# A language-model tower in four blocks: blocks that end without GpSimd's queue drain, and setup's folded weight products reordered

## The reference

```
table = where(is_num, sin(num_value/1000 * freqs), weight);  h = table[x]
q, k, v = split(layernorm(h) @ Wq, @ Wkv)                    # 8 heads of 64
dots = (q k^T) * scale;  dots[diagonal] = -1e-9;  dots = mix(dots, mix_pre)
h = h + (mix(softmax(dots), mix_post) v) @ Wout + bout
y = layernorm(h)
h = h + gelu(y Ws1 + bs1) Ws2 + bs2 + bank_sp(y) + bank_fq(y)  # a bank: top-1 of 8 experts, capacity 1280
```

## Time and profile before

| what | value |
|---|---|
| median of three runs | 1586.62 us |
| the profiled execution | 1587.35 us |
| its span (first to last instruction) | 1585.6 us |
| TensorE busy | 1496.5 us, 94% |
| ScalarE, VectorE, GpSimd busy | 1156.2, 1085.5, 1023.7 us |

### The profile page before, as it was taken

How to read it: one execution, slowest core, us unless ns; L and a number is a source line. 1 busy time by engine, 2 the same in 40 slices (tenths; PEclk the granted TensorE clock), 3 DMA queues, 4 the chain that set the end, 5 groups by cost and what they waited for, 6 DMA issues and landing times. The chain is left out here.

```text
span 1585.6 us, 33983 instructions
## 1 busy us (share of the span) xinstructions
PE 1496.5 (94%) x11213; PEld 1381.3 (87%) x11213; DVE 1085.5 (68%) x2864; ACT 1156.2 (73%) x3447; POOL 1023.7 (65%) x1068
## 2 busy tenths in 40 slices
PE   5549999999999999999999999987999999699999
PEld 2248999999999999999999999977999999699999
DVE  6757787787887887877878787752333333288887
ACT  5539888888888888888888888854555555355554
POOL 5856557878878878878788787663756655422221
PEclk9869999999999999999999999998999999899999
DMA  6323221221211111100000000002334334244444
GB/s 233 131 92 115 96 70 52 69 68 48 59 57 46 56 55 50 46 27 15 14 14 15 15 15 7 4 5 52 83 99 101 84 74 116 64 140 129 131 128 114
DMA packets 157790, 110.59 MB, mean 70 GB/s; under 512 B 28115, under 2 KB 145341, under 8 KB 157616
## 3 DMA queue, kind: packets, MB, share of 16 engines
q1 hardware_dynamic: 140208, 88.25, 18.6%
q0 software_dynamic: 17408, 20.16, 4.6%
HBM read 54.23 MB, written 70.17 MB: 78 GB/s over the span
## 5 line engine op out<-in xcount | busy, mean ns | idle before, releaser
L918 ACT ACTIVATE expd<-masked,nmax 128x128 f32<-128x128 f32 x1024 | 396.0, 393 | 0.0
L729 POOL TENSOR_TENSOR prob<-expd,rtotal 128x1024 f32<-128x1024 f32 x128 | 243.0, 1898 | 143.8 <-DVE rtotal L996 142.9
L1013 DVE COPY_PREDICATED masked<-off_diag,ps_s 128x1024 f32<-128x1024 int32 x128 | 174.9, 1366 | 149.4 <-PE ps_s L816 149.4
L858 PE MATMUL ps_o<-u,probT 128*128 128x128 f32 x2048 | 249.2, 275 | 0.7 <-issue 0.7
L858 PEld LDWEIGHTS ps_o<-u,probT 128*128 128x128 f32 x2048 | 239.1, 192 | 0.9 <-issue 0.9
L918 ACT ACTIVATION_READ_ACCUMULATOR expd<-masked,nmax 128x1 f32 x1024 | 197.0, 192 | 0.0
L927 ACT ACTIVATE u<-ps_ut 128x1024 f32<-128x1024 f32 x128 | 131.4, 1027 | 67.8 <-PE ps_ut L869 67.8
L1028 DVE TENSOR_TENSOR w_lo<-ps_w,w_hi 128x512 fp32r<-128x512 f32 x256 | 164.4, 681 | 5.8 <-ACT w_hi L948 5.8
L941 ACT ACTIVATE probT<-ps_ut 128x1024 f32<-128x1024 f32 x128 | 131.5, 1028 | 45.0 <-PE ps_ut L824 38.3
L948 ACT ACTIVATE w_hi<-ps_w 128x512 fp32r<-128x512 f32 x256 | 146.5, 596 | 19.4 <-PE ps_w L846 12.7
L1019 DVE TENSOR_REDUCE nmax<-masked 128x8 f32<-128x1024 f32 x128 | 155.5, 1214 | 2.5
(11 more groups left out here) (228 smaller groups left out, 4074.9 us busy)
## 6 DMA issues: line engine op xcount, KB each, us to landing
answers_sp<-zeros SPq DMA_DIRECT2D x16, 512.0 KB
answers_fq<-zeros SPq DMA_DIRECT2D x16, 512.0 KB
sh_back<-answers_sp SPq DMA_DIRECT2D x56, 128.0 KB, 2.4
sh_back<-answers_fq SPq DMA_DIRECT2D x56, 128.0 KB, 2.4
out<-res SPq DMA_DIRECT2D x56, 128.0 KB, 1.9
h_sb<-in_L_tok_weight SPq DMA_DIRECT2D x12, 512.0 KB, 5.4
table<-h_sb SPq DMA_DIRECT2D x12, 512.0 KB
sent_sp<-zeros SPq DMA_DIRECT2D x8, 660.0 KB, 3.0
```

The lines of the kernel that those rows point to most:

```text
L729: nc.gpsimd.tensor_tensor(prob[k % 2][:, :].rearrange("p (g j) -> p g j", g=H), expd[k % 2][:, :].rearrange("p (g j) -> p g j", g=H), rtot ...
L858: mm = nc.tensor.matmul(ps_o[:, 0:D], probT[k % 2][:, g * N:(g + 1) * N], u[k % 2][:, g * D:(g + 1) * D], start=(g == 0), stop=(g == H - 1))
L918: ins = nc.scalar.activation(expd[(k - 1) % 2][:, g * N:(g + 1) * N], masked[(k - 1) % 2][:, g * N:(g + 1) * N], ACT.Exp, bias=nmax[(k - 1 ...
L1013: nc.vector.copy_predicated(masked[k % 2][:, :].rearrange("p (g j) -> p g j", g=H), off_diag[:, :].unsqueeze(1).to_broadcast([P, H, N]), p ...
```

## The change

All four blocks are opened with `no_gpsimd_drain=True`. The block's end then has no drain instruction on GpSimd. The other four engines still drain, and then count up the semaphore with an instruction of its own; GpSimd waits for four counts and releases all, as before.

In setup, M is now summed half by half: steps c = 5 to 12 each hold one product of 512 columns instead of steps 5 to 8 holding two, and step 11 no longer holds the first product of N. N's eight products all stand behind the last step, and go to two other accumulators, `ps_t` and `ps_c`, one half in each. They wait for the copy of `ids` out of `ps_c` (made in VectorE's step 6), and no longer for `M_lo`. `M_hi` and `M_lo` move from inside the loops of ScalarE and VectorE to behind them, and `N_hi` and `N_lo` are made in halves of 512 columns.

```
-        block = s.enter_context(nc.Block())
+        block = s.enter_context(nc.Block(no_gpsimd_drain=True))      # in all four blocks

 # ScalarE
-                for w in range(2):
-                    if c == (10, CHUNKS + 1)[w]:
-                        act.wait_ge(S["M"], w + 1)
-                        nc.scalar.activation(mats["MN"[w] + "_hi"][:, :], ps_m[:, :], ACT.Copy).then_inc(S["hi"], 1)
+            act.wait_ge(S["M"], 2)
+            nc.scalar.activation(mats["M_hi"][:, :], ps_m[:, :], ACT.Copy).then_inc(S["hi"], 1)
+            for half, src in enumerate((ps_t, ps_c)):
+                act.wait_ge(S["M"], 3 + half)
+                nc.scalar.activation(mats["N_hi"][:, half * 512:(half + 1) * 512], src[:, :], ACT.Copy).then_inc(S["hi"], 1)

 # TensorE
+            def product(w, c, half):
+                pe.wait_ge(S["wT_out"], 2 + w)
+                pe.wait_ge(S["mixed"], w * HC + c + 1)
+                if w:
+                    pe.wait_ge(S["coef"], 3)
+                dst = (ps_t, ps_c)[half][:, :] if w else ps_m[:, half * 512:(half + 1) * 512]
...
-                if 5 <= c < 5 + HC:
-                    product(c - 5)
-                if c == 11:
-                    product(HC)
-            for c in range(HC + 1, 2 * HC):
-                product(c)
+                if 5 <= c:
+                    product(0, (c - 5) // 2, (c - 5) % 2)
+            for c in range(HC):
+                for half in range(2):
+                    product(1, c, half)

 # VectorE
-                if c == 10:
-                    low(0)
             put_sines(CHUNKS - 2)
             put_sines(CHUNKS - 1)
-            low(1)
+            dve.wait_ge(S["hi"], 1)
+            link.inc(nc.vector.tensor_tensor(mats["M_lo"][:, :], ps_m[:, :], mats["M_hi"][:, :].bitcast(F32), ALU.subtract))
+            for half, src in enumerate((ps_t, ps_c)):
+                at = slice(half * 512, (half + 1) * 512)
+                dve.wait_ge(S["hi"], 2 + half)
+                link.inc(nc.vector.tensor_tensor(mats["N_lo"][:, at], src[:, :], mats["N_hi"][:, at].bitcast(F32), ALU.subtract))
             link.wait()
```

More of the change, by code:

```diff
@@ L281, in setup @@
         names = ("made", "num", "num_f", "numT", "numT_out", "angle", "whole", "reduced", "clamped", "sine", "done", "put",
-                 "weights", "wT", "wT_out", "coef", "coefd", "coef_out", "mixed", "M", "hi", "lo")
+                 "weights", "wT", "wT_out", "coef", "coefd", "coef_out", "mixed", "M", "hi")
         S = {n: sem("s_" + n) for n in names}
@@ L487, in coefficients @@
                 nc.tensor.transpose(ps_c[:, 256:384], idx_f[:, :], ident[:, :]).then_inc(S["coefd"], 1)
[L489 to L502, removed]
+            def product(w, c, half):
[4 more added lines that the diff above has]
+                dst = (ps_t, ps_c)[half][:, :] if w else ps_m[:, half * 512:(half + 1) * 512]
+                ins = nc.tensor.matmul(dst, (wkT, wvT)[w][:, c, :], mixed[:, w * HC + c, half * 512:(half + 1) * 512],
+                                       start=(c == 0), stop=(c == HC - 1))
+                if c == HC - 1:
                     ins.then_inc(S["M"], 1)
@@ L575, in put_sines @@
                                           angle[c % 3][:, 0:n * D].rearrange("p (r d) -> p r d", r=n)).then_inc(S["done"], 1)
[L577 to L580, removed]
             for c in range(CHUNKS):
@@ L587, in _ @@
                     dve.wait_ge(S["coef_out"], 2)
-                    link.inc(nc.vector.tensor_copy(ids[:, :], ps_c[:, 256:384]))
+                    nc.vector.tensor_copy(ids[:, :], ps_c[:, 256:384]).then_inc(S["coef"], 1)
                     dve.wait_ge(S["made"], made["rank_i"])
                     link.inc(nc.vector.tensor_copy(C.rank[:, :], C.rank_i[:, :]))
-                if c == 10:
-                    low(0)
             put_sines(CHUNKS - 2)
             put_sines(CHUNKS - 1)
-            low(1)
+            dve.wait_ge(S["hi"], 1)
[4 more added lines that the diff above has]
+                link.inc(nc.vector.tensor_tensor(mats["N_lo"][:, at], src[:, :], mats["N_hi"][:, at].bitcast(F32), ALU.subtract))
             link.wait()
@@ L669, in attention @@
         s_sent = [sem(f"a_sent{k}") for k in range(8)]
-        block = s.enter_context(nc.Block())
+        block = s.enter_context(nc.Block(no_gpsimd_drain=True))
         def live(i, k):
```

## The result

The median went from 1586.41 us (1584.03 to 1586.75) to 1573.29 us (1570.22 to 1573.91): the ratio of the two is 0.9917 [0.9899, 0.9934], or 13.1 us faster. The forecast was 1571.1 us in a range of 1567 to 1577.2 us. The profiled execution took 1572.82 us against 1587.35 us, 14.5 us less, where 15.5 us were forecast.

The account below looks back on a forecast made before the run. TensorE was taken to bound attention, setup to be a chain with no single bound; only setup and two block ends could change. Savings of 4.2 + 3.9 + 7.4 = 15.5 us off 1586.62 gave 1571.1 us, range 1567 to 1577.2.

Parts of the forecast that it names:

- Attention's end: Between attention and the experts: without the drain the experts' first instruction comes 3.9 us earlier, with 0.45 us for the meeting.
- The term of 7.4 us: At the experts' end: without the drain the meeting is over 0.45 us after GpSimd's last scatter, saving 7.4 us.
- the sign named for this place: Trace sign at the shared network's start: its first row within 0.6 us of GpSimd's last scatter.
- I take nothing for it: Shared network's start: SyncE's wait for the last scatter delays rows read back by some 0.7 us, counted as no cost.
- The lower bound: At the experts' end: 7.4 us less the last scatter's whole landing of 2.1 us, so at least 5.3 us saved.
- Setup: Setup's reordered products: last sines 4.73 us earlier, at 68.5; attention starts near 71.9 instead of 76.48; 4.2 us taken.
- rival A: Setup: N's products run at half clock to the end, setup loses 1.9 us, kernel takes 1577.2 us; chance 0.10.
- up to 0.5 us: Setup's end: GpSimd, the next bound, could hold the last sines back by this much.
- the 71.9 us of the sum: Setup's end: forecast time of attention's start, instead of 76.48, before GpSimd's possible 0.5 us.
- rival B: Experts' start: the shorter gap keeps TensorE's clock from falling, 2.7 us more won, 1568.4 us; chance 0.13.
- The clamps' length: Setup's number loop: GpSimd's clamps stay at 2.06 us though VectorE no longer idles; 0.3 us longer each would cost 1.8 us.
- rival D: Attention: granted clock stays low longer at its start, 7.3 us more per tile, 1593 us with three tiles; chance 0.04.

## Why the prediction was right

**Attention's end: right, in size and reason.** 3.99 us against 3.9. The meeting took 0.35 us where 0.45 were set, and the drain is gone: the same flag at the ends where GpSimd stopped early wins nothing, and a second meeting costs 0.3 us. That GpSimd alone was left to hold the meeting was right. What the prediction did not see, though its numbers have it, is that the time runs from GpSimd's last instruction: 7.8 us here (1094.33 less 1086.55) as at the experts' end, of which VectorE's later end had covered 3.4 us (1089.99 less 1086.55).

**The experts' end: right in its net, wrong in two steps that offset each other.** The term of 7.4 us put the meeting behind GpSimd's last scatter. Without the drain the meeting doesn't wait for scatters that are queued, so 10.2 us were won, and the sign named for this place (the first row within 0.6 us of GpSimd's last scatter) did not come: VectorE began 2.4 us before that scatter was done. The step "I take nothing for it", on the rows that are read back late, failed twice. SyncE's wait was 3.7 us behind the meeting and not 0.7, as the meeting came so early. And the rows are needed not only for the sums at the end of a group, but first for a sum of one tile ahead of the next group's sh_x. In the code it stands there; I had looked at TensorE's first work alone. Together they leave 10.2 - 2.6 = 7.6 us, for a term of 7.4. That two errors of 2.8 and 2.6 us cancel is luck. The lower bound priced the late rows at a whole landing, 2.1 us; they cost more, 2.6 us by the end of the span.

**Setup: right in its chain, a term short by 0.7 us.** VectorE's idle time of 1.17 + 0.27 + 0.45 us went, M_lo left the loop, and the last angles no longer stood behind N. N was summed at 69.65 for a forecast of 70, so rival A did not come. The last sines were 1.34 us later than forecast. The larger part, 0.78 us, is the bound on GpSimd, "up to 0.5 us": I counted its clamps and products, and not the fill that comes with the last steps. The other 0.56 us were lost on VectorE, whose copies of sines the sum took as unchanged and which were longer in three more steps. With the fills moved, attention started at 72.03, close to the 71.9 us of the sum.

**The clock: right in its result, not in its reason.** The gap at attention's end shrank from 7.12 to 3.72 us of TensorE's idle time, and rival B's 2.7 us did not come. The reason against B was that the fall comes 2.4 us after the last matmul, within the shorter gap. It came 4.9 us after, with TensorE already at work for 1.2 us, which is B's own condition. What B had wrong is that the half clock would then be spared: it followed all the same, for 3.4 us in place of 5.4 after TensorE's start, and from its first matmul to VectorE's last result the experts are 0.3 us shorter. So the forecast was right there by luck.

The clamps' length held: 2.05 us with VectorE never idle beside them, against 2.06 us before. But the prediction's contrast with 1.04 us at 17.77 isn't that of VectorE at work or idle. VectorE was at work then too, on its reduce (L566), which reads one tile of SBUF; beside the clamp of 2.06 us stood a copy of sines (L573), which reads two.

Of rival D nothing was seen where it was put, attention's middle is the same. A second fall of the clock showed up at another place, in the shared network's first groups, where TensorE had about 1.9 us more of its work at the lower level.

**What is left.** The 14.5 us of the trace and the 13.1 us of the medians differ by the scatter of single executions, as the profiled one of before lay 0.9 us over its median and that of after 0.5 us under its own. The place of the old setup's end, which moves by 1 us from one execution to another, is a part of that scatter. Attention and the experts were 0.35 and 0.28 us longer; the second follows the rows that TensorE gets 0.6 us later after their issue, and neither was tried.

## What to carry to other kernels

The end of a block costs what the last engine makes it cost: for each engine, read when it stopped, and set that against the next block's first instruction. Here taking out a drain of GpSimd was worth 7.8 us less the time by which GpSimd stopped before the others, and nothing where that was more; where GpSimd stopped last, its queued scatters no longer held the meeting either. When such a wait goes, look at what had been finished in its shelter, here scatters that landed and rows that could be read back, and put work that doesn't need them first.

## What the runs showed of the hardware

- With GpSimd's drain, after a block with indirect DMAs, the next block began 7.8 us after GpSimd's last instruction, in both blocks that sent them and with the transfers landed or not (7.77 to 7.86 us). A second drain with nothing sent since had no cost that shows.
- The meeting of the engines takes 0.28 to 0.36 us at attention's end, and 1.3 us, up to VectorE's first instruction, at the experts' end.
- Without the drain GpSimd goes past a block's end with scatters still queued: two were executed after another engine had begun the next block, the later one 1.4 us after. Whoever reads their result needs a wait of its own, as SyncE has here.
- TensorE's granted clock fell from its full to its lower level 2.3 us after attention's last matmul in the kernel before, with the engine idle, and 4.9 us after it in the kernel after, 1.2 us after the engine had begun again.
